# Expert 2's low weights made behind its gather, list 2 two products ahead, expert 0's second half turned in a bank of its own

## The reference

```python
logits = xn @ router_weight.T + router_bias
probs = jax.nn.softmax(logits, axis=-1)
_, idx = jax.lax.top_k(logits.T, top_k)            # 16 experts x 256 tokens
xe = xn[idx]
h = jnp.einsum('ecd,efd->ecf', xe, fc1_weight) + fc1_bias[:, None, :]
h = jax.nn.gelu(h, approximate=False)
y = jnp.einsum('ecf,edf->ecd', h, fc2_weight) + fc2_bias[:, None, :]
gates = jnp.take_along_axis(probs.T, idx, axis=1)
output = zeros.at[flat_idx].add((y * gates[:, :, None]).reshape(-1, d))
gate_sums = zeros.at[flat_idx].add(gates.reshape(-1, 1))
output = output / gate_sums                        # where a token was chosen
```

## Time and profile before

| | |
|---|---|
| median of 3 runs | 1078.34 us (1076.38 to 1079.67) |
| the profiled execution | 1077.77 us |
| its span, first to last instruction | 1075.9 us |
| PE busy | 975.3 us, 91% |
| DVE busy | 801.7 us, 75% |
| POOL busy | 768.3 us, 71% |
| ACT busy | 675.0 us, 63% |
| PE's mean granted clock | 0.962 of full speed |
| HBM traffic | 66 GB/s over the span |

### The profile page before, as it was taken

The page is one execution under the profiler, slowest core; times in us unless marked ns, Lnnn a source line. Parts: engine busy times, 40 slices in busy tenths (PEclk is TensorE's granted clock), DMA queues, the critical chain, the costliest instruction groups (busy, mean ns, idle before and its releaser), DMA issues. The chain is left out here.

```text
span 1075.9 us, 17837 instructions
## 1 busy us (share of the span) xinstructions
PE 975.3 (91%) x6102; PEld 649.4 (60%) x6102; DVE 801.7 (75%) x1925; ACT 675.0 (63%) x1352; POOL 768.3 (71%) x872
## 2 busy tenths in 40 slices
PE   3899999999999999999998999999821799999995
PEld 3665556555655655665564565444420689999995
DVE  7989688867967886887787678767678767777752
ACT  6875765766777677577756765553445346666662
POOL 4147996798698699779967957899503367777773
PEclk9999999999999999999998999999965699999998
DMA  6020020012012001201110000100246086666652
GB/s 190 1 64 2 6 59 1 1 28 60 1 27 81 1 1 35 74 24 39 46 46 1 4 1 12 42 2 1 62 117 208 21 181 207 208 208 208 207 168 25
DMA packets 73611, 71.82 MB, mean 67 GB/s; under 512 B 38928, under 2 KB 67568, under 8 KB 69424
## 3 DMA queue, kind: packets, MB, share of 16 engines
q1 hardware_dynamic: 66464, 61.92, 18.7%
q0 software_dynamic: 6272, 8.69, 4.7%
q10 hardware_dynamic: 784, 0.07, 0.1%
HBM read 56.83 MB, written 13.83 MB: 66 GB/s over the span
## 5 line engine op out<-in xcount | busy, mean ns | idle before, releaser
L1507 POOL TENSOR_TENSOR prob_sum<-prob_sum,probs 128x256 f32<-128x256 f32 x628 | 467.2, 775 | 79.3 <-ACT probs L1230 70.9
L917 PE MATMUL bank<-probs,v_nat 128*64 128x512 f32 x768 | 190.0, 609 | 0.5 <-ACT probs L1230 0.5
L1822 DVE CUSTOM_DVE_ANT_0 masked_scores<-score_pair,mask_bias 128x512 bf16<-128x512 f32 x142 | 92.1, 686 | 48.6 <-PE score_pair L917 47.2
L1230 ACT ACTIVATE probs<-score_pair,mask_col 128x512 f32<-128x512 f32 x128 | 80.9, 685 | 67.3 <-PE score_pair L917 65.0
L1230 ACT ACTIVATE probs<-pair_bank,mask_col 128x512 f32<-128x512 f32 x128 | 81.1, 689 | 49.4 <-PE pair_bank L917 36.9
L917 PEld LDWEIGHTS bank<-probs,v_nat 128*64 128x64 f32 x768 | 46.0, 136 | 84.2 <-issue 77.6
L1822 DVE CUSTOM_DVE_ANT_0 masked_scores<-pair_bank,mask_bias 128x512 bf16<-128x512 f32 x114 | 73.9, 686 | 25.4 <-PE pair_bank L917 24.0
L1573 POOL DMA_INDIRECT out_x<-y_out,token_index x32 | 54.4, 1699 | 38.7 <-DVE y_out L2142 34.0
L1537 POOL TENSOR_TENSOR w_lo<-w_raw,w_hi 128x1024 fp32r<-128x1024 f32 x28 | 70.3, 2511 | 13.3 <-ACT w_hi L1230 13.1
L1507 POOL TENSOR_TENSOR prob_sum<-probs 128x256 f32<-128x256 f32 x64 | 44.9, 733 | 47.6 <-ACT probs L1230 41.0
L1815 DVE TENSOR_REDUCE maxima<-pair_bank 128x2 f32<-128x1024 f32 x42 | 51.2, 1218 | 25.2 <-PE pair_bank L917 24.9
(11 more groups left out here) (278 smaller groups left out, 2779.7 us busy)
## 6 DMA issues: line engine op xcount, KB each, us to landing
w_raw<-in_fc SPq DMA_DIRECT2D x16, 1024.0 KB, 4.8
w<-in_fc SPq DMA_DIRECT2D x16, 1024.0 KB
c_in<-in_ctx SPq DMA_DIRECT2D x16, 384.0 KB, 4.1
x_in<-in_x SPq DMA_DIRECT2D x8, 512.0 KB, 5.0
out_x<-x_in SPq DMA_DIRECT2D x8, 512.0 KB, 3.9
rows_scratch<-xr_nat SPq DMA_DIRECT2D x8, 512.0 KB, 3.0
c_in<-in_ctx SPq DMA_DIRECT2D x16, 128.0 KB, 4.3
b_rows<-in_fc_bias SPq DMA_DIRECT2D x16, 128.0 KB
```

What stands on the lines that cost most here:

```text
L917: return pe.matmul(out, lhsT, rhs, start=start, stop=stop, skip_group_check=True)
L1230: return act.activation(out, a, f, bias=bias, scale=scale)
L1507: last = tt(total[:, half], first[:, half], p[:, half], ALU.add)
L1822: last = dve.tensor_tensor_reduce(masked_scores[:, hh, :], place[:, hh, :], mask_bias[:, 512 * g:512 * (g + 1)], 1.0, MASKED, ALU.add, ALU ...
```

## The change

Three edits. The low halves of expert 2 leave `split` on POOL and become a piece of their own, `split_low`, behind gather 2 and ahead of `gather_gates(1)`; the high halves on ACT stay. List 2 is counted at point 3 and spread at point 5. The second half of expert 0's tokens is turned in bank 6, and PE no longer waits for the first half's bank.

```diff
     def second_list(at):
-        if at == 5:
+        if at == 3:
             add("list_count", 2)
             add("list_join", 2)
-        elif at == 7:
+        elif at == 5:
             add("list_spread", 2)
             add("gather", 2)
+            for n in range(2):
+                add("split_low", 2, n)
             add("gather_gates", 1)
...
-    turned_bank = xe_bank.rearrange("p (a n) -> p a n", a=2)
+    def turned_place(e, c):
+        return (bank[6] if (e, c) == (0, 1) else xe_bank).rearrange("p (a n) -> p a n", a=2)
...
     for kind, *at in expert_plan:
-        if kind == "split":
+        if kind == "split" and at[0] != 2 or kind == "split_low":
             w_lo_made.will(*at)
...
                 on.wait_ge(gather_done[e % GATHERS], gathers_of(e))
-            if c == 1:
-                on.wait_ge(*xe_emptied.at(*token_key(e, 0)))
...
-                    last = pe.transpose(xe_bank[:, half * CAP + part * P:half * CAP + (part + 1) * P],
+                    last = pe.transpose(turned_place(e, c)[:, half, part * P:(part + 1) * P],
...
         def split(e, n):
+            if e != 2:
+                split_low(e, n)
+
+        def split_low(e, n):
+
             i = e % 2
             on.wait_ge(*w_hi_made.at(e, n))
             if e >= 2:
                 on.wait_ge(*hidden_filled.at(e - 2, FT - 1))
...
-        work = {"split": split, "gather": gather, "gather_gates": gather_gates, "scatter": scatter}
+        work = {"split": split, "split_low": split_low, "gather": gather, "gather_gates": gather_gates, "scatter": scatter}
```

More of the change, by code:

```diff
@@ L1434, in turn_tokens @@
             for half in range(2):
-                last = func(tokens_part(xe_hi[e % 2][:], c)[:, half, :], tokens_part(turned_bank, c)[:, half, :],
+                last = func(tokens_part(xe_hi[e % 2][:], c)[:, half, :], tokens_part(turned_place(e, c), c)[:, half, :],
                             ACT.Identity, scale=nw_col[:, half:half + 1])
@@ L2109, in turn_tokens @@
             for half in range(2):
-                last = stt(tokens_part(xe_lo[i][:], c)[:, half, :], tokens_part(turned_bank, c)[:, half, :],
+                last = stt(tokens_part(xe_lo[i][:], c)[:, half, :], tokens_part(turned_place(e, c), c)[:, half, :],
                            nw_col[:, half:half + 1], as32(tokens_part(xe_hi[i][:], c)[:, half, :]), ALU.mult,
```

## The result

The changed kernel takes 1081.49 us (median of 22 runs, 1079.37 to 1085.22), the kernel before, beside it, 1078.74 (22 runs). The ratio is 1.0029 [1.0019, 1.0038]: slower by 0.29%, some 3 us, at the edge of what counted as a difference in the prediction. The profiled execution of after took 1079.86 us with a span of 1078.1.

A forecast was written before the change was run, and what follows sets the result against it. PE, busy throughout from 894.30 us, was taken as the bound, so expert 3's start decides: - 0.6 us for the start and + 1.7 for the clock give + 1.1, predicted as 1079.1 us, range 1074.6 to 1081.9.

The forecast's parts named there:

- The likeliest case: PE waits for POOL's second low half at expert 3's first product; 1076.3 to 1081.1 us, chance 0.68.
- The third rival: DVE's gate sums stay slow by themselves, so gather 2 starts at 869.4; 2.6 to 4.5 us slower, chance 0.11.
- the freed gate sums: On DVE, no POOL w_lo beside L2055 and L2057, which fall to 0.2 and 0.7 us.
- the wait for POOL at expert 3: PE waits for POOL's w_lo at expert 3's first product, a stall of about 3.5 us.
- Own bank: At PE's turn of expert 0's second half, dropping the wait on xe_lo gives 0 to 0.9 us, taken as 0.1.
- DVE freed by 2.9 us: With POOL quiet, DVE's two gate instructions save 1.2 and 1.7 us, so list 2's ids are ready at 861.9.
- List 2 ahead by 1.9 us: On PE, list 2's count moves from 865.08 to 863.2; spread, index and gather 2 move as far.
- Expert 2's first product: PE wants it at 876.0 instead of 879.25, without waiting for the low halves.
- POOL's arrival at expert 3: POOL's queue, lengthened by 4.66 us of low halves, ends expert 3's second low half at 893.3 to 894.0.
- The step that failed: Late gate rows may stall PE some 1.5 us at list 3's spread, only splitting the stall at expert 3.
- The lock at the new place: Behind gather 2, DVE's last instruction for list 3 may hold POOL, ending the low halves at 875.7 instead of 875.0.
- The clock: The stall at expert 3 brings PE a half clock costing 0, 1.7 or 2.9 us, taken as 1.7.

The follow-up runs named there:

- the held loads: The changed kernel with SP's loads of expert 4's w1 and expert 3's w2 sent only once expert 1's gate rows have landed; 1083.54 us, ratio 1.0034.
- list 2 back: The changed kernel with list 2 counted and spread at points 5 and 7 as before; 1083.58 us, ratio 1.0043.
- gate rows, then low halves: The changed kernel with gather_gates(1) between gather 2 and the low halves of expert 2; 1080.89 us, ratio 1.0014.
- ids behind the turning: The changed kernel with gather_gates(1) right behind gather_gates(0), and list 3's last ids made behind the turning of expert 2's tokens; 1078.20 us, ratio 0.9994.
- the own bank alone: The kernel before with only expert 0's second half turned in a bank of its own; 1077.00 us, ratio 0.9986.

## Why the prediction was right, and where its mechanism and size were off

The range held, from 1074.6 to 1081.9 us. Its mechanism held only up to expert 2. The likeliest case ended at 1081.1, or 2.7 us slower, and the median is 1081.49, 2.75 slower: it is met at its far end, and by a stall at another place. The third rival's span (1080.9 to 1082.8) holds the number too, but its cause is ruled out, since DVE was freed. So the number is right in part by luck. Of the signs that I had named, the freed gate sums, the absent waits at the count and at expert 2's turning and the full clock from 877 to 881 us came; the wait for POOL at expert 3 didn't. By its own steps, after against before:

- **Own bank**, forecast 0.1 us, measured 0.3 to 0.5, and more in the run of that edit alone.
- **DVE freed by 2.9 us**: 0.19 and 0.69 us where I put 0.2 and 0.7. Right.
- **List 2 ahead by 1.9 us**: gather 2 is issued 36.84 us behind the limits instead of 39.53, 2.7 earlier, of which 0.9 is expert 1's earlier start. The count and the turning wait for nothing. Right, but for the 0.26 us at the first spread (list_parts, 863.99).
- **Expert 2's first product** 3.2 us earlier: 3.3 from expert 1 on. Right.
- **POOL's arrival at expert 3**: I had its second low half end at 893.3 to 894.0; it ended at 892.35, which is 893.6 by the marks of before. The number is right, in part by luck: the scatter ahead of it ended 0.6 us earlier than in my sum (889.05, 890.3 by the marks of before, where I had 890.9), and then the low half waited 0.94 us for ACT, which the sum didn't have. It no longer mattered, as PE came at 896.41.
- **The step that failed** is in the paragraph on what hides the rest: "PE may then stall some 1.5 us at the spread of list 3; since it waits for POOL at expert 3 anyway, this only splits the stall". The place and the chain were right (late gate rows, two 1 MB loads, scale_out(1), h_lo, the join). The size was not: 4.26 us. I had given the landing no price of its own (4.8 us instead of 1.3, as the held loads show), nor the lock on the four h_lo behind it, though in the kernel before they took 3.90 us and list_parts stood at 885.79, while my own sum had PE there 4.1 us earlier than 886.40. As PE arrived at expert 3 after POOL, the stall didn't split the one that I had put there but took its place.
- **The lock at the new place** I drew the wrong way round, as 0.7 us that DVE would cost POOL. It was POOL that cost DVE 5.05 us (6.27 for 1.22) and PE 1.36. The Trainium skill's page "SBUF — State Buffer", section "SBUF: two separate sides", says that the pair of ports goes to whichever starts first, for the whole instruction, and by that the DVE instruction, recorded 0.5 us ahead, should have gone first. The trace agrees that the two exclude each other, and by the recorded starts not on who goes first. A row of my own already said so: w_lo<-w began at 894.04, 0.05 us ahead of POOL's w_lo of 894.09, and was the one held, 3.55 us for 1.22.
- **The clock**, forecast 1.7 us for the new stall, was 2.5, and 1.9 in the second trace by the marks. The price was near; it was paid at the spread of list 3 and not at expert 3, and it is most of what the change lost.

From expert 2 to 3 the sum was 15.1 - 0.7 (the half clock of before) + 1.36 + 4.26 + 2.5 = 22.5, measured 22.67; mine was 19.4, with 1.7 of clock and 3.5 of stall. That is 3.3 us too little, of which the earlier experts 0 and 1 gave 0.8 back in these traces. So + 1.1 was forecast for expert 3's start, and + 2.6 came over two traces of each. The direction is that of the forecast case; its mechanism, the wait for POOL at expert 3, didn't occur in after. The experiments show it 0.9 to 3.5 us long in the four kernels with a low half behind gather 2 in which the stall at list 3 is gone.

## What to carry to other kernels

When a piece of work is moved on a queue, ask of each instruction behind it on that queue who waits for its result, and of each transfer that the piece releases what it will travel with; then put a price on the wait that is met first, since it can swallow the one that the sum ends in. When an edit makes one engine earlier, ask of each result that it takes from another engine whether that one comes earlier too: here the join of list 3 didn't, and the time that PE had gained went into a stall, and the clock behind the stall made it a loss. A POOL instruction with SBUF operands is cheap only where DVE has no such work: 4.65 us in POOL's idle time cost the gate sums 2.9 us of DVE time, of which PE waited for 1.8, and the same 4.65 us behind the gather cost the kernel 5 to 6. Parts of a change with different mechanisms should be run apart: two of these three edits made the kernel 0.25% faster, and the third turned that into 0.29% slower.

## What was unexpected of the hardware

- **A DVE instruction recorded ahead of a POOL one is held all the same, and by both of two POOL instructions in a row.** The ids at 867.97 us (after) and 870.59 (list 2 back), each 0.5 us ahead of the first low half, took 6.27 us and ended 1.1 us after the second's end. Their own work is 1.22 us, so nearly nothing of it had been done before the lock. It wasn't let in between the two low halves.
- **Instructions with one SBUF tensor as input were held too**, where I had looked only at those with two: the index's cast of four elements took 2.16 us at 887.81 and ended with the w_lo of 887.54 to 889.94 (gate rows, then low halves), against 0.17; token_in_tile's product took 3.49 us instead of 0.49 (ids behind the turning).
- **A stall of PE doesn't decide the clock by its length.** With the own bank alone the turning of expert 2 waited 2.17 us and the full clock stayed. PE's row:

```profile
874.65 0.66 PE L1177 MATMUL score_pair<-ident,gathered 128*128 128x128 f32 x4 [2.17 <-DMA gathered<-rows_scratch,token_index]
```

The stretches around it, clock in the third column from the end:

```profile
872.00:874.60 2.60, 0.48 (x3) 0.07 (x1) 1.03 (x3) 0.00 (x0) 1.93 (x2) 1.00 0.66 256
874.60:877.00 2.40, 2.35 (x14) 2.14 (x14) 0.78 (x2) 1.65 (x3) 2.10 (x2) 1.00 0.50 54
```

In the kernel before a wait of 1.96 us was followed by 3.4 us at 0.50, and in its second trace one of 2.35 us by a granted clock of 0.56 over the next 3.5. PE's row:

```profile
879.54 1.03 PE L1175 MATMUL score_pair<-ident,gathered 128*128 128x128 f32 x4 [2.35 <-DMA gathered<-rows_scratch,token_index]
```

The stretch behind it:

```profile
880.00:883.50 3.50, 3.50 (x12) 2.91 (x11) 1.95 (x3) 1.78 (x3) 2.73 (x3) 0.56 0.64 67
```

What else decides it stays open.
